# Sixteen samples of attention and graph convolution on one core: input statistics in three batches, marks behind the copy, self weights on the mask's diagonal, small steps moved to ScalarE, and a new order on every queue

## The reference

```python
x = x + L0(_gn(x), ...)      # _gn: group norm over 32 groups of 2 channels
x = x + L1(_gn(x), ...)
# L0: linear attention, 4 heads of 32
qkv = w_qkv @ x;  q = softmax(q, over the 32 of a head) * 32**-0.5;  k = softmax(k, over tokens)
out = w_out @ (context(k, v) applied to q) + b_out
out = (out - mean) * rsqrt(var + 1e-5) * gn_weight + gn_bias      # over the whole sample
# L1: two graph convolutions on a nearest-neighbour graph
xn  = x / norm(x, over channels);  sim = xn @ xn.T                # 1024 x 1024
val, idx = top_k(sim, 9);  v = val / (val.sum() + 1e-6)
out = sum over the 9 neighbours of v * (feat @ w1)[idx] + b1;  silu(group_norm4(out))
out = the same again with w2, b2
```

## Time and profile before

| | us |
|---|---|
| median of 3 runs (687.77 to 695.98) | 694.48 |
| the profiled execution's own time | 693.69 |
| its span, first to last instruction | 691.9 |
| mean granted clock of TensorE, share of full | 0.978 |

### The profile page before, as it was taken

The page is one execution under the profiler, slowest core; times in us unless marked ns, Lnnn a source line. Parts: engine busy times, 40 slices in busy tenths (PEclk is TensorE's granted clock), DMA queues, the critical chain, the costliest instruction groups (busy, mean ns, idle before and its releaser), DMA issues.

```text
span 691.9 us, 12330 instructions
## 1 busy us (share of the span) xinstructions
PE 623.0 (90%) x3821; PEld 312.0 (45%) x3821; DVE 536.2 (77%) x1008; ACT 449.3 (65%) x942; POOL 499.6 (72%) x534
## 2 busy tenths in 40 slices
PE   7787979898999999998999999998989999889984
PEld 5563635344353535353444535353534444333441
DVE  2238788888898989888898889898888988857821
ACT  2236658586786878585867768786858687643321
POOL 0122787868787888888797978888887979786810
PEclk9999999999999999999999999999999999979997
DMA  3002343434354444435353535435343634454311
GB/s 93 0 17 46 71 83 78 91 71 107 83 102 84 100 85 93 92 83 102 76 110 77 108 76 107 85 86 103 83 96 71 108 63 101 82 96 88 62 32 31
DMA packets 148722, 55.76 MB, mean 81 GB/s; under 512 B 138008, under 2 KB 138512, under 8 KB 148656
## 3 DMA queue, kind: packets, MB, share of 16 engines
q1 hardware_dynamic: 148656, 54.97, 38.8%
HBM read 12.87 MB, written 4.32 MB: 25 GB/s over the span
## 4 chain that ended last, share of the span: by engine, by line
PE 31%; POOL 25%; issue 16%; DVE 10%; DMA 9%; ACT 7%; SPq 1%; POOLq 0%; ACTq 0%; DVEq 0%
PE pC L967 17%; POOL adj L389 10%; POOL adj L384 5%; PE pS L923 4%; DMA rbc<-rn_row 4%; DMA rn_row<-rnT 4%; POOL qn L348 3%; ACT adj L527 2%; PE pB L768 2%; POOL res L407 2%; DVE kstat L607 2%; ACT ek L458 2%; PE pA L807 2%; POOL xn L372 2%; DVE top L676 2%
## 5 line engine op out<-in xcount | busy, mean ns | idle before, releaser
L967 PE MATMUL pC<-adj,xt 128*64 128x512 f32 x992 | 233.2, 603 | 3.1 <-POOL adj L395 1.8
L389 POOL TENSOR_TENSOR adj<-maskT,adj 128x128 f32<-128x128 f16 (+3 forms) x127 | 163.6, 1288 | 28.2 <-DMA maskT<-mask 25.3
L676 DVE MAX8 top<-pS 128x8 f32<-128x1024 f32 x128 | 155.6, 1224 | 30.7 <-ACT adj L527 30.5
L694 DVE MATCH_REPLACE8 mask<-top,pS 128x1024 uint16<-128x1024 f32 x128 | 155.3, 1213 | 0.0
L923 PE MATMUL pS<-xn 64*128 64x512 f32 x256 | 145.3, 655 | 6.2 <-issue 5.6
L923 PE MATMUL pS<-xn,xsw 64*128 64x512 f32 x256 | 144.7, 656 | 2.9 <-DVE mask L694 2.9
L527 ACT COPY adj<-pS 128x1024 f32<-128x1024 f32 x128 | 128.3, 1004 | 27.3 <-PE pS L925 27.1
L384 POOL TENSOR_TENSOR adj<-maskT,adj 128x128 f32<-128x128 f16 (+6 forms) x111 | 128.5, 1158 | 0.0
L967 PEld LDWEIGHTS pC<-adj,xt 128*64 128x64 f32 x992 | 63.9, 137 | 103.6 <-issue 96.0
L395 POOL TENSOR_TENSOR adj<-adj,selves 128x128 f32<-128x128 f32 x127 | 58.7, 462 | 8.7
L925 PEld LDWEIGHTS pS<-mark,place 64*128 64x128 f16 x256 | 24.5, 96 | 76.1 <-issue 76.1
(11 more groups left out here) (153 smaller groups left out, 1101.7 us busy)
## 6 DMA issues: line engine op xcount, KB each, us to landing
xs<-x SPq DMA_DIRECT2D x32, 128.0 KB, 2.8
vbc<-v_row SPq DMA_DIRECT2D x32, 128.0 KB, 2.9
rbc<-rn_row SPq DMA_DIRECT2D x30, 128.0 KB, 2.8
xsw<-xn SPq DMA_DIRECT2D x30, 128.0 KB, 2.4
out<-res SPq DMA_DIRECT2D x30, 128.0 KB, 2.4
maskT<-mask SPq DMA_TRANSPOSE x128, 3.1
cst<-packed SPq DMA_DIRECT2D x1, 471.5 KB, 3.9
y1sw<-y SPq DMA_DIRECT2D x2, 128.0 KB, 2.3
```

What stands on the lines that cost most here:

```text
L389: pool.tensor_tensor(above, m[:, r, 0:r + 1, :].bitcast(F16), above, ALU.mult).then_inc(done["upper"], 1)
L676: dve.max(top[b % 2][:, r, 0:TOP], pS[r % 2][:, :]).then_inc(done["tile_top"], 1)
L694: dve.match_replace(out=mask[n % MASKS][:, :], in_to_replace=top[b % 2][:, r, 0:TOP], in_values=pS[r % 2][:, :], imm_value=ONE_BITS).then_ ...
L967: mm = pe.matmul(ps[h * C:(h + 1) * C, 0:H], xt[:, t % NJ, t // NJ, :], adj[b % 2][:, t, h * H:(h + 1) * H], start=(t == 0), stop=(t == NT ...
```

## The change

Seven things are changed at once:

1. **Input statistics in three batches** (`BATCHES = [0, 1, 8]`: sample 0, samples 1 to 7, samples 8 to 15). The stage `inputs` does them on VectorE (statistics per sample; then, once per batch, spread, deviations, squares, variance and bias), with one mean matmul and one power on GpSimd per batch. Samples 1 to 15 are loaded once more at the start for it, by four DMAs into `early`, which is the memory of `adj[1]`.
2. **Marks behind the copy.** The mark matmuls leave `similarity` and become a stage `marks`, which waits for the copy; `top` waits for `marked` where it waited for `sim_copied`. So the copy in `adj` holds the diagonal as it is.
3. **Self weights on the mask's diagonal.** `itself`, `selves` and the addition are gone. Before `U`, GpSimd sets the diagonal of the transposed mask to one.
4. **Affine steps on ScalarE**: `plain` and `affine`, which made scale and bias of each norm on VectorE, are now ScalarE's; so are the copies `rnT`, `mT` and `vrT`. The factor `SCALE` moves into `u`.
5. `exchange` is a stage of its own (only sample 0 has work in it).
6. **New order**: new TIMES, and three rows of BEGINS, one for each of three groups of stages.
7. A new `WARM`: the counts are others, and some places too.

```diff
+PARTS = {"inputs": 0, "attend": 0, "unit": 0, "exchange": 0, "weights": 1, "itself": 1, "neighbours": 1, "tops": 1, "masks": 1, "marks": 1, "convolve": 2}
...
-                    live += [(BEGINS[b] + at, steps) for at in TIMES[engine][stage.__name__]]
+                    live += [(BEGINS[PARTS[stage.__name__]][b] + at, steps) for at in TIMES[engine][stage.__name__]]
...
+            for first, end in zip(BATCHES[1:], BATCHES[2:] + [B]):
+                for h in range(2):
+                    sp.dma_start(early[h * C:(h + 1) * C, first:end, :],
+                                 x[first:end, :, h * H:(h + 1) * H].rearrange("b c n -> c b n")).then_inc(done[f"x_early{BATCHES.index(first)}"], 16)
...
                     pool.wait_ge(*of_buffer("turned", n, MASKS, 16))
-                    pool.wait_ge(*of_tile("sim_copied", n))
+                    own = m[:, r, r, :].bitcast(F16)
+                    pool.affine_select(out=own, in_=own, compare_op=ALU.not_equal, fill=1.0, base=0, pattern=[[-1, P]],
+                                       channel_multiplier=1).then_inc(done["diagonal"], 1)
...
                     pool.tensor_tensor(above, m[:, r, 0:r + 1, :].bitcast(F16), above, ALU.mult).then_inc(done["upper"], 1)
-                    yield
-
-                    pool.wait_ge(*of_tile("upper", n))
-                    pool.wait_ge(*of_tile("self_ready", n))
-                    own = a[:, r, r * P:(r + 1) * P]
-                    pool.tensor_tensor(own, own, selves[:, r, :], ALU.add).then_inc(done["diagonal"], 1)
...
+            def plain(b, tag):
+
+                act.wait_ge(*of(f"{tag}_rstd", b))
+                act.activation(st[tag][:, 15:16], st[tag][:, 9:10], ACT.Copy, scale=st[tag][:, 13:14]).then_inc(done[f"{tag}_bias"], 1)
+
+            def affine(b, tag, weight, bias):
+                t = st[tag]
+                act.wait_ge(*of(f"{tag}_rstd", b))
+                act.activation(t[:, 14:15], t[:, 13:14], ACT.Copy, scale=weight).then_inc(done[f"{tag}_scale"], 1)
+                act.wait_ge(*of(f"{tag}_scale", b))
+                act.activation(t[:, 15:16], t[:, 9:10], ACT.Identity, bias=bias, scale=t[:, 14:15]).then_inc(done[f"{tag}_bias"], 1)
...
-            def itself(b):
-                for r in range(NT):
-                    yield
-                    act.wait_ge(*of("ss_read", b, 2))
-                    act.wait_ge(*of_tile("diagonal", NT * (b - 1) + r))
-                    act.activation(selves[:, r, :], ident, ACT.Copy, scale=top[b % 2][:, r, TOP:TOP + 1]).then_inc(done["self_ready"], 1)
...
+                    if b == 1 and r == 0:
+                        act.wait_ge(done["in_stat"], 2 * B)
...
+            def inputs(b):
...
+                    for i in range(first, end):
+                        yield
...
+                        dve.bn_stats(in_stats[:, i, :], xs[i][:, :] if k == 0 else early[:, i, :]).then_inc(done["in_stat"], 1)
+                        dve.wait_ge(done["in_stat"], 2 * i + 1)
+                        dve.bn_aggr(in_spread[:, i, 4:6], in_stats[:, i, :]).then_inc(done["in_stat"], 1)
...
-                    dve.wait_ge(*of_tile("sim_copied", n))
+                    dve.wait_ge(*of_tile("marked", n))
...
-            def attend(b):
-                yield
-                warm("in_mean", b)
-                pe.wait_ge(*of("at_veps", b - 1))
-                average(b, "in", pB, "avg_pair")
...
+            def input_means(k):
+                first, end = (BATCHES + [B])[k:k + 2]
+                pe.wait_ge(done["in_spread"], k + 1)
+                pe.matmul(pB[:, 0:6 * (end - first)], const("avg_pair"), in_spread[:, first:end, :], start=True,
+                          stop=True).then_inc(done["in_mean_ps"], 1)
...
+            def mark(b, r):
+                n = NT * b + r
+                own, _ = token_block(r)
+                pe.wait_ge(*of_tile("sim_copied", n))
                 for s in range(2):
                     mm = pe.matmul(pS[r % 2][:, r * P + s * C:r * P + (s + 1) * C], place16[own, s, :], mark16[own, :], start=False,
                                    stop=True, skip_group_check=True)
-                mm.then_inc(done["sim_ps"], 1)
+                mm.then_inc(done["marked"], 1)
```

More of the change, by code:

```diff
@@ L74 @@
 WARM = {
-    ("start", 0): 36, ("k", 0): 20, ("ekT", 0): 9, ("qT", 0): 8, ("att", 0): 7, ("at_mean", 0): 16, ("in_mean", 1): 6,
-    ("mi_mean", 0): 32, ("k", 1): 9, ("ss", 0): 4, ("att", 1): 6, ("sim1", 0): 2, ("mi_mean", 1): 24, ("k", 2): 9,
-    ("xt1", 1): 24, ("g1_mean", 14): 18, ("sim7", 15): 12, ("g2_mean", 14): 18, ("g1_mean", 15): 12, ("xt2", 15): 21,
-    ("a2_0", 15): 5, ("ky", 0): 20,
+    ("start", 0): 36, ("k", 0): 28, ("ekT", 0): 9, ("qT", 0): 10, ("att", 0): 8, ("at_mean", 0): 3, ("yT", 1): 10,
+    ("mi_mean", 0): 37, ("ss", 0): 25, ("att", 1): 4, ("sim4", 0): 11, ("sim5", 0): 23, ("xt1", 1): 18, ("sim0", 1): 16,
+    ("att", 2): 5, ("sim7", 15): 16, ("xt2", 14): 19, ("g1_mean", 15): 4, ("xt2", 15): 30, ("a2_0", 15): 4, ("ky", 0): 18,
 }
@@ L178, in build @@
         top = [sb(f"top{i}", [P, NT, TOP + 2]) for i in range(2)]
-        selves = sb("selves", [P, NT, P])
+        early = adj[1][:, :, :].rearrange("p t (s n) -> p (t s) n", s=2)
         vtot = sb("vtot", [P, NT])
@@ L500, in unit @@
                 yield
+                plain(b, "mi")
+                yield
                 act.wait_ge(*of("mi_bias", b))
@@ L922, in similarity @@
                     src = xn if r // NJ == h else xsw
-                    pe.matmul(pS[r % 2][:, h * H:(h + 1) * H], src[b % 2][c, rows], xn[b % 2][c, :], start=True, stop=True)
+                    mm = pe.matmul(pS[r % 2][:, h * H:(h + 1) * H], src[b % 2][c, rows], xn[b % 2][c, :], start=True, stop=True)
+                mm.then_inc(done["sim_ps"], 1)
+            def mark(b, r):
+                n = NT * b + r
+                own, _ = token_block(r)
+                pe.wait_ge(*of_tile("sim_copied", n))
                 for s in range(2):
@@ L942, in neighbours, with marks @@
                     similarity(b, r)
+            def marks(b):
+                for r in range(NT):
+                    yield
+                    mark(b, r)
             def aggregate(b, xt, signal):
```

276 lines of the change are left out of this document (164 added, 112 removed).

## The result

| | before | changed |
|---|---|---|
| median, us | 693.64 | 786.97 |
| range, 4 runs of each | 687.77 to 695.98 | 781.61 to 789.95 |
| span of the profiled execution | 691.9 | 782.6 |
| mean granted clock of TensorE | 0.978 | 0.921 |
| mean period, xt1(2) to xt1(15) | 37.89 | 43.46 |

The ratio is 1.135, 95% interval 1.130 to 1.140: 93 us slower. The time predicted was 762, the range 726 to 800.

The account below looks back on a forecast made before the run. TensorE was taken as the bound, busy for 35.69 of 37.49 us. 693.7 + 53 (thirteen periods at +4.1) + 3.7 (sample 15) + 11.8 (start) = 762 us, range 726 to 800.

Parts of the forecast that it names:

- the two adjacencies: `g2mean` right behind `a2_7` on TensorE; second aggregation's read and statistics ahead of `top0` on VectorE: 4.9 us waiting with `at_mean`, for 0.54.
- The period's size: Time per sample on TensorE: 35.4 work + 4.9 new waits + 1.5 other waits = 41.8 against 37.7, +4.1 us.
- the rest of the period: TensorE's waits outside the second aggregation's end, such as for `qn`, `D` and ScalarE's small copies: left at 1.5 us.
- the clock's case: Rival: TensorE's clock also falls behind each sample's pauses, 1.5 to 3 us per period, 794 us; chance 0.20.
- the 0.9 of my sign: Sign for the clock rival: granted clock under 0.9 in the middle of the changed kernel.
- The pause of 1.65 in the earlier trace: Kernel before: the matmul at 129.10 behind this single pause took 0.66, as usual, so one pause need not lower the clock.
- the pause ahead of `sim2`: Sign: TensorE pauses 2.7 to 4 us there each sample, released by VectorE's mask; if missing, the prediction is wrong altogether.
- All this is worth nothing by itself: Lighter GpSimd, ScalarE and VectorE (3.7 us per sample) bring nothing, since none of these engines is the bound.
- The start: First similarity +11.8 us: `qsum(0)` +7.9 from statistics ahead of it, `qT(1)` ahead of `sim0(0)` +3.9; early loads off the path.
- The dense rest: Rival: stalls take the other waits' place, period 35.4 + 4.9 = 40.3, 742 us; chance 0.18.
- Faster: Rival: GpSimd's loop sets the period and gets lighter, period 35.9, -1.8 each, about 679 us; chance 0.09.
- The end: Sample 15, aggregation ahead of its own `sim2`: +4.1 less 0.4 for its last tile's lost addition, 3.7 us in the sum.

Follow-up runs that it names:

- x_warm: Changed kernel in its order, with 28 multiplications of zeros in TensorE's pause ahead of `g2mean`, samples 2 to 14: 776.2 us median, ratio 1.122.
- x_pe: Changed kernel with `att` and `g2mean`, `k` put back behind `a2_7` and `sim2` on TensorE, ScalarE's copy of `att` ahead of the spread: 803.4 us, one run.
- x_best: Changed kernel, both adjacencies undone from sample 2, first tile's mark ahead of `qT(b+1)`, start in the old order: 703.9 us median, ratio 1.016.

## Why the prediction was right, and where it was not

**The bound and the place.** Right. The thirteen periods bring 72 of the 91 us, and the two adjacencies named are what they come from: taken out they give back 56 us (4.3 of the 5.6 per period), put into the kernel before they cost 93, and one alone gives back next to nothing. The steps, in the period at 400.78: `a2_7` through at 7.0 (7.1 predicted), the pause for `g2mean` 3.7 (2.7 and 1.2 for the copy of `att`, 3.9), the first mask at 12.1 (12.4).

**The period's size.** 5.6 where I had 4.1, and these 1.5 in thirteen periods are 19 of the 25 us between 762 and 787. At the full clock the sum came out: the common period of x_warm is 41.6 for 41.8. That is in part luck, since two terms were off and cancel: TensorE's work is 35.8 and not 35.4, and the rest of the period waits for 1.0 and not 1.5 (the two adjacencies for 4.8, predicted 4.9). Two terms were missing. One is the clock's case, to which I gave 0.20: it came beside the forecast and not in its place, granted 0.89 to 0.96 in twelve periods (0.93 on average, so above the 0.9 of my sign; in the last it is 0.81, where the kernel before has 0.87) and 0.79 in the 16 us around the pause. I had priced it at 1.5 to 3 per period on top; it cost 0.8, since `k` and `sim2` at half speed filled waits that I had counted in full. The pause of 1.65 in the earlier trace rows, from which I argued that one pause need not do it, said nothing about pauses of 3.7. The other 0.7 are periods longer than the common one, which the sum has no term for. In x_warm there are waits of 0.5 to 1.2 us ahead of `sim0` in six of its periods, for which the profile names no releaser, and two falls of the clock; the kernel before has such periods too (38.9 and 38.7 among 37.3, with 1.5 to 1.7 us of waiting for `qn`). What brings them stays open.

**The signs.** I had written that I am wrong altogether if the pause ahead of `sim2` is missing, and it is missing in eight of thirteen periods. The sign was wrong and not the mechanism: my own sum has TensorE through with `g2mean` and `k` at 12.3 and the mask at 12.4, so it leaves 0.1 us of waiting there, not the 2.7 to 4 of the sign. The pause stands ahead of `g2mean`; ahead of `sim2` it opens when `g2mean` is moved away (4.33 in x_pe). VectorE idled for 7.0 and not 5 ahead of the read.

**Work off the critical queue.** The prices of the single steps were near: the diagonal write 0.293 (0.35 predicted, 0.20 to 0.46), the affine steps 0.286 and 0.387 (about 0.30 each), the statistics 0.66. The sum for VectorE was not: it is lighter by 2.6 per period, where I had 3.7. TensorE lost 0.27 with the input's mean for my 0.35. Two of my readings are not as the rows have them, without weight for the sum: the 0.205 of an affine step is line 593's and stands in no row, and two maxima and a mask take 2.37 and 1.21 in the earlier trace rows, not 2.28 and 1.27. "All this is worth nothing by itself" did not hold. In the old order the affine steps and the copies moved with them cost 0.87 per period, in the main because a table load came out of its cover, and I had only costed the steps: at most 0.1 per norm. The marks with the diagonal cost 1.9 there; I had 0.1, for the matmuls alone, and had not asked who waits for a mark. The marks apart cost TensorE 0.4 in the new order (35.84 for the 35.42 of the batches alone) and 0.7 in the old one, inside the bounds of 0 and 0.8, but not the 0.1 in the sum. The new order hides most of the waits: with its faults repaired its mean period is 38.5, where the old order has 40.4 with the same work and 37.9 without. It loads silu's table for `y3`, far ahead of `y2` (changed kernel, ScalarE; `y2` needs no load of its own):

```profile
425.24 1.28 ACT L584 ACT_TABLE_LOAD   x1
426.53 0.81 ACT L584 ACTIVATE y<-g,st_g 128x512 f32<-128x512 f32 x1
```

**The start.** The first similarity was at 67.5 (67.0 predicted): right, but by luck, since three errors cancel. `qsum(0)` lost 8.9, not 7.9, 1.6 of it a wait for the early loads, which I had put beside the path. `qT(1)` held the first similarity by 6.3 behind `xt1(0)`, with its own time at half speed, not by 3.9; and from `qsum(0)` to `xt1(0)` 2.9 less passed than before, where I had no change. And the step matters less than I said, for no gain of taking it out reached sample 2. Of the 11.6 I can show only that the start as a whole cost them (places, zeros and guards): with all of it put back in x_best `xt1(1)` is at 84.1 in place of 98.2.

**The rivals.** The dense rest (742) is out as a whole: the rest of the period kept 1.0 of its 1.5 us of waits. Faster (679) had its ground in GpSimd's loop; a GpSimd lighter by 1.8 per period gained about 0.3, a sixth of the 1.8 that the rival needed. The end: 6.7 behind `xt1(15)` where I had 3.7.

## What to carry to other kernels

- A step in an in-order queue is priced by what stands behind it and by the queue that feeds it. Two adjacencies that each wait for the other engine hide each other: undone one by one they show next to nothing or a loss (784, 803 for 787), together 56 us. When one repair shows nothing, look what is next in line before dropping it.
- Before moving a small step to another engine, look at what ran while its result was waited for. Here it was a table load of 1.28 us, longer than the two steps together (0.67).
- Less work is not less time, and an order tuned by hand fits only the work it was tuned for: the same new work gave 731 in the old order, 787 in the new one and 704 in the new one with eight steps moved in each period and the start put back.

## What the runs showed of the hardware that I had not expected

- The clock fell behind pauses much shorter than those of the earlier trace rows. In the repaired kernel it was at 1.00 from 325 to 342, and TensorE was busy for 16.7 of these 17 us. Then it waited 0.40 and 0.43 us, and the queries' matmuls behind the second wait took 2.04, where 1.16 is usual; a third wait of 0.44 came when the clock had already fallen. The granted clock was 0.76 from 338 to 352, and that period was 41.3 us long instead of 37.9:

```profile
342.41 0.38 PE L902 MATMUL pB<-spread_g,cst 128*128 128x34 f32 x2 [0.40 <-ACT spread_g L529]
343.21 2.04 PE L943 MATMUL pA<-cst,y 64*128 64x128 f32 x16 [0.43 <-ACT ekT L580]
...
346.00 1.98 PE L997 MATMUL pB<-ekT,yT 128*64 128x128 f32 x16 [0.44 <-ACT rnT L634]
```

Four periods later the same three waits stand, of the same lengths, and the clock did not fall. The first two of them (same kernel and view):

```profile
498.09 0.38 PE L902 MATMUL pB<-spread_g,cst 128*128 128x34 f32 x2 [0.40 <-ACT spread_g L529]
498.89 1.16 PE L943 MATMUL pA<-cst,y 64*128 64x128 f32 x16 [0.43 <-ACT ekT L580]
```

What decides stays open.

- A multiplication of 128x7 values on VectorE took 1.92 us, where its neighbours of 128x7 took 0.15 to 0.18. It ran while GpSimd multiplied 128x1024 values, and ended with it (changed kernel, VectorE, then GpSimd):

```profile
33.32 1.92 DVE L683 TENSOR_TENSOR in_bias<-in_minus,in_rstd 128x7 f32<-128x7 f32 x1
```

```profile
33.30 1.91 POOL L376 TENSOR_TENSOR qn<-qe,qrec 128x1024 f32<-128x1024 f32 x1
```

  The Trainium skill (SBUF — State Buffer, SBUF: two separate sides) says that a VectorE instruction with two inputs from SBUF and a GpSimd instruction that reads SBUF exclude each other for their whole length. The trace agrees; in the run with the batches alone the same instruction took 1.22, beside an addition of 1.26 on GpSimd. There it held nothing, since the statistics behind it need that addition's result.
